# First tile in two halves, a weight load behind a gather, and constant products between routing steps, in a one-core graph and expert layer

## The reference, cut to what matters

```python
xn = _layernorm(x, axis=-1)                      # x: 1250 x 1024, float32
x = x + _L0_gnn_ref(xn, W, a, src, dst) + _L0_mix_ref(xn[None], wql, wqr, wk, wv)[0]
x = x + _L0_ffn_ref(_layernorm(x, axis=-1)[None], gate_W, gate_b, expert_W, expert_b)[0]
# mix: ((xn wql) * (xn wqr)) @ ((xn wk)^T (xn wv))
# gnn: segment sums over 20000 edges of exp(-leaky_relu(al[src] + ar[dst])) * h[dst]
# ffn: 8 experts, the best 2 per row by softmax of gate scores, weighted and halved
```

## Time and profile before

| | us |
|---|---|
| median of 3 runs | 1233.85 |
| lowest, highest | 1231.38, 1236.93 |
| the profiled execution | 1235.77 |
| its span in the trace | 1234.0 |
| PE busy in the span | 1182.7 |
| DVE busy | 746.4 |
| ACT busy | 308.8 |
| POOL busy | 453.8 |
| mean granted clock of PE | 0.979 |

### The profile page before, as it was taken

How to read it: one execution, slowest core, us unless ns; L and a number is a source line. 1 busy time by engine, 2 the same in 40 slices (tenths; PEclk the granted TensorE clock), 3 DMA queues, 4 the chain that set the end, 5 groups by cost and what they waited for, 6 DMA issues and landing times.

```text
span 1234.0 us, 16278 instructions
## 1 busy us (share of the span) xinstructions
PE 1182.7 (96%) x5799; PEld 995.7 (81%) x5799; DVE 746.4 (60%) x1509; ACT 308.8 (25%) x415; POOL 453.8 (37%) x434
## 2 busy tenths in 40 slices
PE   6989999999999999999999999999966999999996
PEld 5888888878788989888887888888855788888884
DVE  7889622454334577777767447998476822553434
ACT  2421212223121111111011122333251611432333
POOL 3950577878786000000000006224232534444343
PEclk9999999999999999999999999999976999999998
DMA  6111442741421322211146652242276965685744
GB/s 209 35 35 35 112 129 70 263 144 42 131 53 37 90 90 90 90 56 56 39 119 190 193 163 69 106 176 105 99 274 240 356 128 85 197 279 108 203 91 75
DMA packets 91031, 156.08 MB, mean 126 GB/s; under 512 B 14786, under 2 KB 45244, under 8 KB 90836
## 3 DMA queue, kind: packets, MB, share of 16 engines
q1 hardware_dynamic: 75556, 129.76, 31.1%
q0 software_dynamic: 15408, 25.44, 11.5%
HBM read 112.95 MB, written 42.04 MB: 126 GB/s over the span
## 4 chain that ended last, share of the span: by engine, by line
PE 86%; DVE 9%; DMA 2%; issue 1%; ACT 1%; POOL 0%; DVEq 0%; POOLq 0%; ACTq 0%
PE ps L1628 26%; PE ps L1629 26%; PE ps L1630 26%; PE ps L1756 2%; PE ps L1870 2%; DVE e_lo L1453 2%; PE ps L1799 2%; DVE run L1098 1%; PE ps L1715 1%; DVE xn_lo L1076 1%; DVE stats L1050 1%; DMA gx<-xn_d,tok_of 1%; DVE acc L1065 1%; DMA gx<-xn_d,tok_now 1%; PE ps L1668 1%
## 5 line engine op out<-in xcount | busy, mean ns | idle before, releaser
L700 POOL DMA_INDIRECT tab_d<-val_i,addr_i x160 | 207.0, 1294 | 110.5 <-issue 110.5
L1628 PE MATMUL ps<-e_hi,lt_hi 128*128 128x512 f32 x368 | 148.0, 402 | 2.4 <-DVE e_lo L1453 2.1
L715 POOL TENSOR_TENSOR att_part<-att 128x640 f32<-128x640 f32 x10 | 15.8, 1576 | 364.3 <-PE ps L1630 350.9
L1630 PE MATMUL ps<-e_hi,lt_lo 128*128 128x512 f32 x368 | 144.1, 392 | 0.0
L1629 PE MATMUL ps<-e_lo,lt_hi 128*128 128x512 f32 x368 | 144.0, 391 | 0.0
L1628 PE MATMUL ps<-xt_hi,q_hi 128*128 128x416 f32 (+1 forms) x384 | 142.0, 370 | 0.0
L1629 PE MATMUL ps<-xt_lo,q_hi 128*128 128x416 f32 (+1 forms) x384 | 135.3, 352 | 0.0
L1630 PE MATMUL ps<-xt_hi,q_lo 128*128 128x416 f32 (+1 forms) x384 | 134.9, 351 | 0.0
L1286 DVE TENSOR_TENSOR cnt<-ps,cnt 128x256 f32 x208 | 87.1, 419 | 39.1 <-PE ps L1756 24.0
L804 POOL DMA_INDIRECT out<-y,row_put x46 | 74.0, 1608 | 86.5 <-ACT y L1008 45.8
L1628 PEld LDWEIGHTS ps<-e_hi,lt_hi 128*128 128x128 f32 x368 | 69.5, 189 | 22.6 <-DVE e_lo L1453 8.9
(11 more groups left out here) (293 smaller groups left out, 2673.9 us busy)
## 6 DMA issues: line engine op xcount, KB each, us to landing
e_raw<-in_L_ffn_expert_W SPq DMA_DIRECT2D x64, 512.0 KB, 11.0
acc<-in_x SPq DMA_DIRECT2D x18, 512.0 KB, 8.2
w_raw<-in_L_mix_w_key SPq DMA_DIRECT2D x16, 512.0 KB
h_d<-hs SPq DMA_DIRECT2D x18, 256.0 KB
q_in<-q_d SPq DMA_DIRECT2D x9, 512.0 KB, 5.2
xm<-in_x SPq DMA_DIRECT2D x18, 256.0 KB
h_in<-h_d SPq DMA_DIRECT2D x9, 512.0 KB, 5.8
mix_d<-xm SPq DMA_DIRECT2D x18, 256.0 KB
```

The lines of the kernel that those rows point to most:

```text
L700: nc.gpsimd.indirect_dma_start(out=tab_d, out_offset=bass.IndirectOffsetOnAxis(ap=addr_i[0:EP, j:j + 1], axis=0), in_=val_i[0:EP, j:j + 1] ...
L1628: nc.tensor.matmul(o, lh, rh, start=(k == 0), stop=False)
L1630: return nc.tensor.matmul(o, ll, rh, start=False, stop=(k == last_k))
```

## The change

It has four parts.

1. Tile 0 is normed, cast and subtracted in two halves of 512 columns, PE waits by halves, and `norm_stats(1)` stands behind `xn_lo` of tile 0.
2. SP waits for the first gather (`s_gx` of 16) ahead of the transfers of expert 2.
3. PE runs 38 products of two constants (`ident` and `ones`, float32, 128 by 128, into a PSUM bank that nobody reads) in five places of the routing: 14 behind the last gate, 4 behind the count products, 6 among the reads of `bounds`, 8 among the reads behind L1862's product and 6 after them. The reads change too: four ahead of the token products instead of six (the first bound is the constant 0), four behind them.
4. `FIRST_LO` is 4 instead of 3: rows of expert 0 and 1 that ACT and DVE split ahead of the routing and the first block.

```diff
+        XN_PARTS = [[(0, HALF), (HALF, D)]] + [[(0, D)]] * (NT - 1)
+        XN_COUNT = [sum(len(p) for p in XN_PARTS[:t]) for t in range(NT)]
-        FIRST_LO = 3
+        FIRST_LO = 4
@@ SP
+            sp.wait_ge(s_gx, 16)
             load_expert(2, range(KB))
@@ ACT
-                act.wait_ge(s_xn, t + 1)
-                nc.scalar.copy(xn_hi[0:ROWS[t], t, :], acc[0:ROWS[t], t, :]).then_inc(s_xhi, 1)
+                for p, (lo, hi) in enumerate(XN_PARTS[t]):
+                    act.wait_ge(s_xn, XN_COUNT[t] + p + 1)
+                    nc.scalar.copy(xn_hi[0:ROWS[t], t, lo:hi], acc[0:ROWS[t], t, lo:hi]).then_inc(s_xhi, 1)
@@ DVE
             for t in range(NT):
                 normalise(t)
-                if t + 1 < NT:
+                if 1 <= t and t + 1 < NT:
                     norm_stats(t + 1)
...
+                for p, (lo, hi) in enumerate(XN_PARTS[t]):
+                    dve.wait_ge(s_xhi, XN_COUNT[t] + p + 1)
+                    nc.vector.tensor_tensor(xn_lo[0:w, t, lo:hi], acc[0:w, t, lo:hi], xn_hi[0:w, t, lo:hi].bitcast(f32),
+                                            ALU.subtract).then_inc(s_xlo, 1)
+                if t == 0:
+                    norm_stats(1)
@@ PE
+            SPARE = gnn_sum(NT - 1) % NB
+            pe.wait_ge(*released(gnn_sum(NT - 1)))
+            def keep_busy(times):
+                for _ in range(times):
+                    nc.tensor.matmul(ps[:, SPARE, 0:P], ident[:, :], ones[:, :], start=True, stop=True)
...
             gate(NT - 1)
+            keep_busy(14)
             pe.wait_ge(s_gtot, 1)
...
+            keep_busy(4)
             pe.wait_ge(s_bounds, 1)
-            first_block = [pe.value_load(bounds[0:1, e:e + 1], min_val=0, max_val=NBLK) for e in range(6)]
+            first_block = [0]
+            for e in range(1, 5):
+                first_block.append(pe.value_load(bounds[0:1, e:e + 1], min_val=0, max_val=NBLK))
+                keep_busy(1 + e % 2)
...
-            for e in range(6, NE + 1):
+            for e in range(5, NE + 1):
                 first_block.append(pe.value_load(bounds[0:1, e:e + 1], min_val=0, max_val=NBLK))
+                keep_busy(2)
+            keep_busy(6)
```

More of the change, by code:

```diff
@@ L1064, in normalise @@
                 link(nc.vector.tensor_tensor(rstd[0:w, t:t + 1], nt1[0:w, :], nt2[0:w, :], ALU.mult))
-                nc.vector.tensor_scalar(acc[0:w, t, :], acc[0:w, t, :], mean[0:w, t:t + 1], rstd[0:w, t:t + 1],
-                                        ALU.subtract, ALU.mult).then_inc(s_xn, 1)
+                for lo, hi in XN_PARTS[t]:
+                    nc.vector.tensor_scalar(acc[0:w, t, lo:hi], acc[0:w, t, lo:hi], mean[0:w, t:t + 1], rstd[0:w, t:t + 1],
+                                            ALU.subtract, ALU.mult).then_inc(s_xn, 1)
             norm_stats(0)
@@ L1071, in _ @@
                 normalise(t)
-                if t + 1 < NT:
+                if 1 <= t and t + 1 < NT:
                     norm_stats(t + 1)
                 w = ROWS[t]
-                dve.wait_ge(s_xhi, t + 1)
-                nc.vector.tensor_tensor(xn_lo[0:w, t, :], acc[0:w, t, :], xn_hi[0:w, t, :].bitcast(f32),
-                                        ALU.subtract).then_inc(s_xlo, 1)
+                for p, (lo, hi) in enumerate(XN_PARTS[t]):
[4 more added lines that the diff above has]
+                    norm_stats(1)
                 if t == 2:
@@ L1643, in _ @@
             for t in range(NT):
-                pe.wait_ge(s_xlo, t + 1)
                 for i in range(NB):
+                    m, lo, w = G_PIECES[i]
+                    for p, (start, _) in enumerate(XN_PARTS[t]):
+                        if start < max((m + 1) * P, lo + w):
+                            pe.wait_ge(s_xlo, XN_COUNT[t] + p + 1)
                     gram_piece(i, t)
@@ L1842, in _ @@
             rows_transposed(NT - 2)
+            SPARE = gnn_sum(NT - 1) % NB
+            assert SPARE in (0, 1, 3)
+            pe.wait_ge(*released(gnn_sum(NT - 1)))
+            def keep_busy(times):
+                for _ in range(times):
+                    nc.tensor.matmul(ps[:, SPARE, 0:P], ident[:, :], ones[:, :], start=True, stop=True)
             gate(NT - 4)
```

## The result

The changed kernel takes 1230.24 us, median of 20 runs (1226.47 to 1233.22), where the kernel before took 1234.2 (1229.2 to 1237.33) beside it: a ratio of 0.997, with a 95% interval of 0.9961 to 0.998, or 4.0 us less. The forecast was 1226.7, a gain of 7.2 us. It has the sign and about twice the size.

The account below looks back on a forecast made before the run. PE bounds all but the start, where DVE leads, and the routing, with its waits and half clock. +0.8 + 0.1 - 9.1 + 0.5 + 0.5 = -7.2 us: 1228.6 from the profiled execution, forecast 1226.7 against the median, range 1223 to 1232.

Parts of the forecast that it names:

- Part 1, +0.8: Start: halving tile 0 starts PE earlier but delays DVE, so the mirror transposes come 0.8 us later (0.4 to 1.3).
- Part 2, -4.5: Routing: with expert 2 held back, the first gather falls from 8.35 to 3.85 us, -4.5 (-2 to -5).
- even-sharing rival: First gather: evenly shared engines cost only some 1.25 us, so 3.2 of its 8.35 stay; 1229.9 us, chance 0.07.
- Part 4, 0: Ahead of the routing: one more row split by DVE and cast by ACT in waits, counted as 0 alone.
- Part 3, the counts, +0.4 - 0.3, and the tokens, -0.7: Routing: constant products cost 0.44 or 0.22 us each; counts 0.4 late, 0.3 given back; token products fall 1.43 to 0.7.
- Left half, 4.6 from the clock and the tokens: Block 0: left half ends at 940.0 instead of 949.05, -9.1 us, 4.6 of it from clock and token products.
- Collisions, +0.5 and +0.5: Second and third gathers meet expert 2's load: +0.5 us (0 to 3) and +0.5 us (0 to 2).
- The clock that does not hold: Rival, routing: clock falls again, last 14 constant products start at half clock; -5.0 us, 1228.9, chance 0.22.
- The collisions' number, 1230.2: Rival: second gather waits for expert 2, third for expert 3, +3 and +1.5; in all -3.7 us, chance 0.17.
- The slower case: Rival, routing: constant products at half clock throughout delay what follows; at 0.6 each +5.3 us, about 1239; chance 0.08.
- signs to look for: First product near 9.5, first gather below 4.5, clock 1.00 from 922 to 945, left half near 941, second gather ending PE's wait.
- signs of being wrong: Mirror transposes before 82.5, first gather above 6 us, constant products over 1.5 late, half clock at first block, long later gather waits.

Follow-up runs that it names:

- e1: The changed kernel again, with no edit: 1230.5 us against 1233.39 for the kernel before, ratio 0.9975.
- e3: The changed kernel without SP's wait for the first gather ahead of expert 2: 1233.79 us, ratio 0.9999 to the kernel before.
- e6: The kernel before with only the 38 constant products and the changed reads: 1230.52 us, ratio 0.9973 to the kernel before.
- e9: The changed kernel with FIRST_LO back at 3: 1229.83 us against 1234.63 for the kernel before, ratio 0.9962.
- e17: e16 with FIRST_LO 4: 1229.52 us against 1234.68 for the kernel before, ratio 0.9958.
- e16: e15 with tok_w laid out so that the columns of a weight-sum product lie side by side: 1228.54 us, ratio 0.9959 to the kernel before.
- e8: The changed kernel without halves, with more constant products in the last four gates, token products and weight sums: 1233.2 us, ratio 0.9994 to the kernel before.
- e2: The changed kernel with tile 0 in one piece, without the halves: 1230.53 us, ratio 0.997 to the kernel before.
- e11: The kernel before with SP's wait and all 38 constant products, no halves, FIRST_LO 3: 1229.65 us, ratio 0.9959 to the kernel before.
- e4: The changed kernel without the constant products, reads still split: 1230.11 us, ratio 0.9969 to the kernel before.
- e12: e11 with 10 constant products instead of 14 ahead of the counts and 10 instead of 14 behind the reads: 1228.42 us, ratio 0.995 to the kernel before.
- e15: e12 again: 1228.63 us against 1234.19 for the kernel before, ratio 0.9962.
- e18: The changed kernel a third time, beside e17: 1229.92 us, ratio 0.9968 to the kernel before.
- e5: The kernel before with only SP's wait ahead of expert 2 added: 1229.58 us against 1234.71, ratio 0.9954.
- e10: e5 again: 1230.34 us, ratio 0.9962 to the kernel before.

## Why the prediction was right or wrong

**What bounds the kernel.** Right. The stretches that it named are those that moved by more than the kernel's own spread, and the 284.0 to 285.4 us behind the second transposes stayed.

**Part 1, +0.8.** Right in kind and nearly in size. PE's first product stood at 9.33, and DVE was 0.7 later at tile 9. DVE's timeline of tile 0 and the first step of tile 1, where the earlier trace rows stood before:

```profile
7.35 1.00 DVE L1070 TENSOR_SCALAR acc<-acc,mean,rstd 128x512 f32<-128x512 f32 x2
8.58 1.29 DVE L1082 TENSOR_TENSOR xn_lo<-acc,xn_hi 128x512 fp32r<-128x512 f32 x2 [0.23 <-ACT xn_hi L840]
...
11.90 0.16 DVE L1065 RECIPROCAL nt<-sdx 128x1 f32<-128x1 f32 x1 [0.34 <-ACT sdx L837]
```

The two waits that the step counted are there, 0.23 for the cast and 0.34 for the root. At the mirror transposes 0.6 is left on average (82.76 against 82.18). One profile would have said -0.5 (82.03), since DVE waited 1.3 us less for a weight transfer (0.18, against 1.46 in the first profile of before).

**Part 2, -4.5.** The step held: 4.4 to 4.8 us from issue to transposes in all profiles with the wait but e1, 4.5 on average, against 8.37: -3.9. The forecast had taken 3.85 for the quiet gather, from the second one; the first takes 0.7 more. The even-sharing rival (7 in 100) is out: with the load 7.69 and 7.64 in e3 and e6, without it 4.5, so the load costs 3.2 where even sharing would cost 1.25. The Trainium skill's rule in "DMA: Bandwidth & Descriptors", Queues, rings and completion order, by which an engine takes turns between the queues, is the ground of that rival; neither these numbers nor the second gather's 9.9 us agree with an even share.

**Part 4, 0.** Not told from 0 (e9; and e17 against e16).

**Part 3, the counts, +0.4 - 0.3, and the tokens, -0.7.** The price, 0.44 and 0.22, held (6.15 us for 14 at half clock in e1; in e8, at full clock, what follows such a product starts 0.24 behind it, 936.17 to 936.41). The delay was 0 to 1.3 us by when the clock rose; in the six profiles with all 38 products and the wait (the changed kernel's three, e2, e9, e11) the counts stood 7.86 behind the last gate, +0.5. From there to the issue of the gather they took 7.56 instead of 8.22, -0.7, of -1.0 forecast; in e4, with the reads split and no products, it is 8.01, so the split reads give 0.2 of it. The token products themselves gained nothing, 1.54 against 1.41: their columns too lie 40 bytes apart.

**Left half, 4.6 from the clock and the tokens.** This is the step that failed. It said: transposes 0.9, weight sums 1.6, left half 5.5, DVE last at 940.0, so 8.65 us from the first transposes to the second (931.35 to 940.0), where before had 12.47 (12.19 on average). Measured with the clock up in the left half: 10.0 (the changed kernel's three profiles). Two things keep it from 8.65. The weight sums took 3.37 and not 1.6: with them the forecast's own terms for PE, 0.9, 3.37, 0.25 and 5.5, give 10.0. The step had halved them with the clock, and no row showed them at full clock. And the second gather, issued 1.3 to 1.4 us behind the first transposes, was used 8.6 to 8.7 us later: by that alone the second transposes stand 10.0 behind the first. PE and the gather were ready within 0.15 us of each other, so faster weight sums alone would have won nearly nothing, and e16 and e17 won nothing with them. Where the clock fell at the end of the weight sums it took 11.3 to 11.5 (e2, e9, e11), a gain of 0.7 to 0.9 instead of 3.8. From the windows of e2, while PE ran the weight sums and then the first products of block 0:

```profile
935.00:936.00 1.00, 1.00 (x8) 0.89 (x7) 1.00 (x2) 0.00 (x0) 0.00 (x0) 1.00 0.97 365
936.00:937.00 1.00, 1.00 (x14) 0.91 (x13) 1.00 (x2) 0.00 (x0) 0.00 (x0) 0.92 0.76 287
937.00:938.00 1.00, 1.00 (x3) 0.81 (x4) 1.00 (x2) 0.00 (x0) 0.00 (x0) 0.50 0.94 360
```

Of ten profiles with constant products in the waits only and the old weight sums, nine show a fall between 921 and 938; only the changed kernel's first one has none. In five of them it fell around the token products (e1, e3, e12, e15, e18), in seven between the start of the weight sums and the first microsecond of block 0 (e2, e3, e6, e9, e11, e12, e15). The constant products did lift the clock: in one of the microseconds 918 to 920, where without them (e4, e5, e10) it stayed at 0.50 to 940 or later. But it fell again before it was used, and then the next constant products cost double. That the narrow products let it fall is likely and not shown. All seven profiles with a fall at the weight sums had PE idle for 0.9 to 4.2 us ahead of the transposes; in e1 and e18 no wait stood there, and the clock, which had just come back, outlasted the same weight sums. But the first profile had such a wait too, 1.11, and no fall. The Trainium skill says in "TensorE: Matmul & The Clock Gate", What's actually happening, that the moment at which the clock rises varies from run to run of the same kernel; the profiles of the changed kernel agree, with a rise in 918, 920 and 918 under constant products begun at 914.65, 915.62 and 915.18. The fall moved more: none, one at 927, one at 928.

**Collisions, +0.5 and +0.5.** The second gather's own time was foreseen well: 8.6 to 8.7 us from issue to use in the changed kernel, 8.35 in the forecast. But it cost PE only about 0.1 us, since the weight sums had made PE late too: the weight load of the second transposes waited 0.33, 0.42 and 0.39 for it, and PE started them 0.07 to 0.15 later than the pace of its products. Where PE comes earlier, as in e17, it is the next bound. The third gather ended no wait of PE in the changed kernel; in e16 it did, 1.19. The fourth did, for 0.7 to 1.1 us, in single profiles of before, e2, e3, e8 and e10 alike; these and e16 are the six with 284.8 us or more behind the second transposes.

**The sum.** By the six profiles the terms are +0.6, +0.5, -0.7, then -3.7 for the gather (4.71 on average, e1's delay in it) and -1.5 for the last stretch (10.7): -4.7 before rounding, against 3.6 measured and 7.2 forecast. What is left is within the spread of executions: the runs of either kernel lie within 7 to 8 us, and the three profiled runs of the changed kernel (1227.49, 1230.48, 1228.20) lie 1.5 below its median.

**The rivals.** The clock that does not hold (22 in 100, 1228.9) is nearest to what happened: it had the clock down again when the last 14 products ran, as in five of the ten profiles, and not the fall at the weight sums, which seven show. Its time came out 1.3 below the measured one; it too took the quiet gather for 3.85 and had no price for weight sums that stay at 3.37. The collisions' number, 1230.2, fits by chance: its +3 for the second gather was 0.1. The slower case needed a clock that is never lifted; what it said of late products came true in parts (e1).

**Of the signs to look for**, the first product at 9.5, the gather at 4.5, the transposes in 0.9 and the left half near 941 (941.6 to 944.5) were there. The clock at 1.00 from 922 to 945 was there in one profile of ten, and the second gather released only the weight load. Of the signs of being wrong, mirror transposes earlier than 82.5 were there in two of three profiles (82.03, 82.34), by the spread, though the term was right.

**What stays open.** What the products are worth: by comparisons -3.3 (e6 against before), -0.1 (e3, with halves), +0.1 (e11 against the wait alone), +0.2 (changed against e4), while the profiles give them 1.5 us from the last gate to the second transposes (30.8 on average in the six, 32.3 in e4, e5 and e10). The wait's worth depends on the pair too: 5.2 alone, 3.0 with everything else in place (e1 against e3), and 1.7 beside the products (e11 against e6, on different chips, with intervals that overlap). So it is shown that the wait pays, and not how much of it is left where the products are. It is open why e6 and e3, 3.2 us apart in time, differ by 1.9 in their spans, with no more than 0.6 for the halves. And what makes the clock fall in the routing is open.

## What to carry to other kernels

A load that nobody needs soon should be issued behind the small transfer on which everything waits, and then the next small transfer is to be looked at. Filler products can pay only if they fit the wait at the lower clock too, and if the clock that they lift is still up when the work comes that gains by it. A forecast from one profile should not count the moments at which the clock rises or falls as fixed.

## What the runs showed of the hardware

- Weight sums whose moving columns lie apart took the same time at either clock: 20 products of 87 columns, 40 bytes from one to the next, 3.37 us at 1.00 and 3.38 at 0.50. Side by side they took 1.40 at 1.00 (e16) and 1.68 at 0.50 (e17). The Trainium skill says in "SBUF — State Buffer", Specifications (TRN2), that SBUF has lines of 16 bytes and that each step to a new line costs extra; the runs agree.
- DVE has the price on its side: 1.21 us for three tables of 580 elements read and written along, 3.38 read across.
- A granted clock of 1.00 fell to 0.50 in a microsecond in which PE was listed as busy throughout. In before it did so in 907, under gate products of 8 columns, with PE listed as busy in every microsecond from 892 on. It also did under 20 products of 29 columns (e1, 927) and under 20 of 87 (e9, 937), there behind waits of 0.36 and 1.09 us. It did not in e8, where constant products stood among them.
- A gather of 512 KB took 4.5 us from its issue to its use in quiet, 7.6 to 8.4 behind a load, and 8.6 to 9.9 when it was issued amid a load of 4.2 MB (the second gather of the changed kernel and of e17).
